# Token choice: eight rounds of the eight largest on one row per batch, norms on ScalarE, heads' weights on SP's queue

## What is computed

```python
hs = layernorm(x)                                   # (4, 512, 512)
scores = einsum('btd,d->bt', hs, w_router)
_, idx = top_k(scores, 64)                          # 64 tokens of each batch
idx = sort(idx)
sel = hs[b, idx]                                    # 256 rows in all
processed = transformer_layer(sel, rope at idx)     # 16 query heads, 8 key heads, MLP
gated = sigmoid(scores[b, idx]) * processed + (1 - sigmoid(...)) * sel
x = x + hs.at[b, idx].set(gated)
```

## Time and profile before

| what | us |
|---|---|
| median of 3 executions | 2518.43 |
| lowest, highest | 2517.94, 2521.67 |
| profiled execution: time | 2518.06 |
| profiled execution: span, first to last instruction | 2516.1 |
| busy in the span: TensorE, VectorE, ScalarE, GpSimd | 1986.4, 1068.8, 530.5, 1147.9 |
| mean granted TensorE clock | 0.893 of full speed |

### The profile page before, as it was taken

How to read it: one execution, slowest core, us unless ns; L and a number is a source line. 1 busy time by engine, 2 the same in 40 slices (tenths; PEclk the granted TensorE clock), 3 DMA queues, 4 the chain that set the end, 5 groups by cost and what they waited for, 6 DMA issues and landing times.

```text
span 2516.1 us, 33335 instructions
## 1 busy us (share of the span) xinstructions
PE 1986.4 (79%) x10460; PEld 1427.2 (57%) x10461; DVE 1068.8 (42%) x2094; ACT 530.5 (21%) x1132; POOL 1147.9 (46%) x578
## 2 busy tenths in 40 slices
PE   6925887968845789986762599999999999999910
PEld 3413443433312333333751599999999999999910
DVE  2573442057664667753840243333333333333300
ACT  3300221101102455441110121121122112112200
POOL 0000000003552655553357204776855878781886
PEclk8966997989975899999885799999999999999965
DMA  3052003221124444542135112555544545552999
GB/s 106 0 152 80 15 27 116 93 76 51 67 83 129 152 147 159 165 151 60 46 141 207 60 44 73 179 156 161 181 157 149 176 153 188 172 183 76 204 159 192
DMA packets 200086, 307.42 MB, mean 122 GB/s; under 512 B 16673, under 2 KB 95153, under 8 KB 199761
## 3 DMA queue, kind: packets, MB, share of 16 engines
q1 hardware_dynamic: 129744, 180.77, 22.6%
q0 software_dynamic: 21504, 50.74, 8.9%
q10 hardware_dynamic: 48768, 74.98, 8.9%
HBM read 188.33 MB, written 118.10 MB: 122 GB/s over the span
## 4 chain that ended last, share of the span: by engine, by line
PE 40%; issue 5%; POOL 5%; DMA 1%; DVE 1%; ACT 0%; SPq 0%; POOLq 0%; DVEq 0%; ACTq 0%
PE psum L2122 15%; PE psum L2142 8%; PE psum L2127 8%; POOL X L1748 5%; PE psum L2147 4%; PE psum L2109 3%; PE psum L2116 2%; DMA X<-d_y,f_slots 1%; DVE r_score L1915 1%; PE psum L2080 0%; PE psum L2072 0%; DMA r_w_gate<-in_L_ffn_gate_w 0%; DVE r_score L1916 0%; DVE e_gu_low L1886 0%; ACT r_hot L1767 0%
## 5 line engine op out<-in xcount | busy, mean ns | idle before, releaser
L2122 PE MATMUL psum<-e_gu_high,e_rowT_high 128*128 (+1 forms) x1272 | 430.1, 340 | 10.3 <-issue 10.2
L2122 PE MATMUL psum<-e_gu_low,e_rowT_high 128*128 (+1 forms) x1272 | 412.1, 326 | 4.0 <-issue 4.0
L1775 ACT ACTIVATE e_silu<-psum 128x352 f32<-128x352 f32 x159 | 74.0, 466 | 961.0 <-PE psum L2127 850.4
L2127 PE MATMUL psum<-e_gu_high,e_rowT_low 128*128 (+1 forms) x1272 | 258.7, 325 | 22.2 <-DVE e_rowT_low L1843 12.8
L2122 PEld LDWEIGHTS psum<-e_gu_high,e_rowT_high 128*128 128x128 f32 x1272 | 241.4, 190 | 31.5 <-issue 26.8
L2122 PEld LDWEIGHTS psum<-e_gu_low,e_rowT_high 128*128 128x128 f32 x1272 | 242.5, 191 | 8.6 <-issue 4.3
L1685 POOL TENSOR_TENSOR e_gu_high<-e_gu_in,e_ones 128x1408 fp32r<-128x1408 f32 x33 | 83.7, 2536 | 323.4 <-PE psum L2127 315.9
L2127 PEld LDWEIGHTS psum<-e_gu_high,e_rowT_low 128*128 128x128 f32 x1272 | 215.3, 190 | 23.2 <-DVE e_rowT_low L1843 13.1
L2142 PE MATMUL psum<-e_d_high,e_midT_high 128*128 (+3 forms) x477 | 190.4, 399 | 46.5 <-issue 45.6
L1852 DVE TENSOR_TENSOR e_midT_low<-psum,e_midT_high 128x256 fp32r<-128x256 f32 x159 | 67.5, 425 | 350.8 <-ACT e_midT_high L1784 323.0
L2142 PE MATMUL psum<-e_d_low,e_midT_high 128*128 (+3 forms) x477 | 189.4, 397 | 0.0
(11 more groups left out here) (338 smaller groups left out, 3693.6 us busy)
## 6 DMA issues: line engine op xcount, KB each, us to landing
d_sorted<-y_zeros SPq DMA_DIRECT2D x32, 1040.0 KB, 8.6
d_y<-e_y ACTq DMA_DIRECT2D x127, 256.0 KB
e_row<-d_sorted ACTq DMA_DIRECT2D x125, 260.0 KB
e_gu_in<-in_L_ffn_w_gate SPq DMA_DIRECT2D x32, 704.0 KB, 4.4
e_gu_in<-in_L_ffn_w_up SPq DMA_DIRECT2D x32, 704.0 KB, 5.1
e_d_in<-in_L_ffn_w_down SPq DMA_DIRECT2D x32, 512.0 KB, 4.4
d_y<-y_zeros SPq DMA_DIRECT2D x8, 1024.0 KB, 5.5
e_d_in<-in_L_ffn_w_down SPq DMA_DIRECT2D x32, 192.0 KB, 4.9
```

The lines of the kernel that those rows point to most:

```text
L2122: nc.tensor.matmul(bank[:, 0:M].unsqueeze(1), rowT_high[par][:, k, :], w[:, bass.ds(buffer, 1), k, at:at + M], start=(k == 0 and n == 0), ...
L2127: last = nc.tensor.matmul(bank[:, 0:M].unsqueeze(1), rowT_low[par][:, k, :], gu_high[:, bass.ds(buffer, 1), k, at:at + M], start=False, st ...
```

## The change

- VectorE makes one more small step, `shift` = -mean times root. ScalarE then makes the sixteen normed tiles, as X times root plus shift, and signals each; VectorE makes the score of each tile as it comes. The products' unused output goes to the eight banks and to eight parts of SBUF tables that are written later.
- The scores are turned by four transposes into one row of 512 per batch, on 4 partitions. VectorE copies the rows twice, then eight times takes the eight largest of each row (`max`) and overwrites them (`match_replace`). What differs from the copy is chosen; a scan counts the chosen, one product adds the base of the batch and clears the others. Four transposes turn the slots back, a copy of 16 columns follows, and the one-hot table is made as before.
- The trip of the scores through DRAM, the tables `before` and `tri` of this stage, the counting of larger and equal scores and the two small products are gone.
- The additions X + hs move behind the one-hot table.
- The heads' weights are issued by SP, behind the constants, without a wait.

In the diff the declarations of tiles and semaphores are left out, and some of the removed lines, which stand in the code above.

```diff
             @block.sync
             def _(sp):
                 sp.dma_start(w_router[:], c.dram["L0_ffn_w_router"].partition_broadcast(P)).then_inc(router_loaded, 16)
-                for dst, src in ((before[:], c.dram["i_before"]),
-                                 (tri[:], c.dram["i_tri"]), (iota[:], c.dram["i_iota"]), (slot_base[:], c.dram["i_slot_base"]),
+                for dst, src in ((slot_base[:], c.dram["i_slot_base"]), (iota[:], c.dram["i_count"]),
                                  (rope[:], c.dram["i_rope"].rearrange("(j p) d -> p j d", p=P)),
                                  (ln_w[:, 0], c.dram["L0_ffn_ln1_w"].rearrange("(k p) -> p k", p=P)),
                                  (ln_w[:, 1], c.dram["L0_ffn_ln2_w"].rearrange("(k p) -> p k", p=P))):
                     sp.dma_start(dst, src, allow_slow_non_contiguous=True).then_inc(loaded, 16)
-                sp.wait_ge(score_T_ready, 1)
-                sp.dma_start(c.dram["d_scores"], score_T[:]).then_inc(score_stored, 16)
-                sp.wait_ge(score_stored, 16)
-
-                sp.dma_start(scores_of_batch[:], c.dram["d_scores"].rearrange("(b j) p -> (b j p)", b=B).partition_broadcast(P)
-                             .rearrange("q (b s) -> q b s", b=B)).then_inc(scores_spread, 16)
+                for k in range(CC):
+                    rows = slice(k * P, (k + 1) * P)
+                    for src, at, cols in ((c.dram["L0_ffn_wq"], 0, QH * DH), (c.dram["L0_ffn_wk"], QH * DH, DH),
+                                          (c.dram["L0_ffn_wv"], (QH + 1) * DH, DH)):
+                        sp.dma_start(w_heads[:, k, :, at:at + cols],
+                                     src[rows, :].rearrange("p (h n) -> p h n", n=cols)).then_inc(heads_loaded, 16)
...
-                nc.gpsimd.memset(ones[:], 1.0)
+                nc.gpsimd.memset(ones[:], 1.0).then_inc(ones_set, 1)
...
                 norm_rows_into(nc, dve, chain, c, mv, rstd, var_ready, rstd_ready, 1e-5)
+                nc.vector.scalar_tensor_tensor(shift[:], mv[:, :, 0], -1.0, rstd[:], ALU.mult, ALU.mult).then_inc(shift_ready, 1)
                 dve.wait_ge(router_loaded, 16)
-                with dve.Fori(0, B) as b:
-                    tiles = [bass.ds(b * JT + j, 1) for j in range(JT)]
-                    for t in tiles:
-                        last = nc.vector.tensor_scalar(hs[:, t, :], c.X[:, t, :], mv[:, t, 0:1], rstd[:, t],
-                                                       ALU.subtract, ALU.mult)
...
-                dve.wait_ge(score_turned, 1)
-                nc.vector.tensor_copy(score_T[:], c.bank[0][0:NT, 0:P]).then_inc(score_T_ready, 1)
...
-                dve.wait_ge(scores_spread, 16)
...
-                    of_batch = scores_of_batch[:, bass.ds(b, 1), :]
-                    for j in range(JT):
-                        t = bass.ds(b * JT + j, 1)
-                        nc.vector.tensor_scalar(c.bank[j][:].unsqueeze(1), of_batch, score[:, t], None, ALU.is_gt,
-                                                ALU.add, accum_out=above[:, t])
-                        last = nc.vector.scalar_tensor_tensor(c.bank[4 + j][:].unsqueeze(1), of_batch, score[:, t],
-                                                              before[:, j:j + 1, :], ALU.is_equal, ALU.mult,
-                                                              accum_out=equal[:, t])
-                    last.then_inc(chain_dve, 1)
...
-                chain.link(nc.vector.tensor_tensor(slot[:], c.bank[1][:, 0:NT], slot_base[:], ALU.add))
-                chain.link(nc.vector.tensor_tensor(slot[:], slot[:], chosen[:], ALU.mult))
-                chain.link(nc.vector.tensor_scalar(slot[:], slot[:], -1.0, None, ALU.add))
+                unread = [bank[:] for bank in c.bank]
+                unread += [held[:, 4 * q:4 * q + 4, :].rearrange("p t s -> p (t s)") for held in (slot_hot, slot_hot_T) for q in range(4)]
+                for t in range(NT):
+                    dve.wait_ge(row_ready, t + 1)
+                    last = nc.vector.scalar_tensor_tensor(unread[t], hs[:, t, :], 1.0, w_router[:], ALU.mult, ALU.mult,
+                                                          accum_out=score[:, t:t + 1])
+                last.then_inc(score_ready, 1)
+
+                dve.wait_ge(scores_turned, 1)
+                nc.vector.tensor_copy(of_batch[:], c.bank[0][0:B, :])
+                chain.link(nc.vector.tensor_copy(left[:], c.bank[0][0:B, :]))
+                for n in range(CAP // 8):
+                    chain.link(nc.vector.max(best[:, n, :], left[:]))
+                    chain.link(nc.vector.match_replace(left[:], best[:, n, :], left[:], -3e38))
+                chain.link(nc.vector.tensor_tensor(picks[:], left[:], of_batch[:], ALU.not_equal))
+                dve.wait_ge(ones_set, 1)
+                chain.link(nc.vector.tensor_tensor_scan(slot_rows[:], ones[:], picks[:], 0.0, ALU.mult, ALU.add))
+                dve.wait_ge(loaded, 5 * 16)
+                nc.vector.scalar_tensor_tensor(slot_rows[:], slot_rows[:], slot_base[:], picks[:], ALU.add, ALU.mult).then_inc(slots_found, 1)
+
+                dve.wait_ge(slots_turned, 1)
+                chain.link(nc.vector.tensor_copy(slot[:].rearrange("p (b j) -> p b j", j=JT),
+                                                 c.bank[1][:, 0:NT].rearrange("p (j b) -> p b j", b=B)))
                 nc.vector.tensor_tensor(slot_hot[:], iota[:].unsqueeze(1).broadcast_to((P, NT, P)),
                                         slot[:].unsqueeze(2).broadcast_to((P, NT, P)), ALU.is_equal).then_inc(hot_ready, 1)
+                for t in range(NT):
+                    nc.vector.tensor_tensor(c.X[:, t, :], c.X[:, t, :], hs[:, t, :], ALU.add)
                 dve.wait_ge(gathered, 1)
...
             @block.scalar
             def _(act):
-                for k in range(CC):
-                    if k == CC // 2:
-
-                        act.wait_ge(scores_spread, 16)
-                    rows = slice(k * P, (k + 1) * P)
-                    for src, at, cols in ((c.dram["L0_ffn_wq"], 0, QH * DH), (c.dram["L0_ffn_wk"], QH * DH, DH),
-                                          (c.dram["L0_ffn_wv"], (QH + 1) * DH, DH)):
-                        act.dma_start(w_heads[:, k, :, at:at + cols],
-                                     src[rows, :].rearrange("p (h n) -> p h n", n=cols)).then_inc(heads_loaded, 16)
+                act.wait_ge(rstd_ready, 1)
+                act.wait_ge(shift_ready, 1)
+                for t in range(NT):
+                    nc.scalar.activation(hs[:, t, :], c.X[:, t, :], ACT.Identity, bias=shift[:, t:t + 1],
+                                         scale=rstd[:, t:t + 1]).then_inc(row_ready, 1)
                 act.wait_ge(gate_ready, 1)
...
             @block.tensor
             def _(pe):
-                pe.wait_ge(score_ready, B)
-                nc.tensor.transpose(c.bank[0][0:NT, 0:P], score[:], c.ident[:]).then_inc(score_turned, 1)
-
-                pe.wait_ge(chosen_ready, 1)
-                nc.tensor.matmul(c.bank[1][:, 0:NT], tri[:], chosen[:], start=True, stop=False)
-                nc.tensor.matmul(c.bank[1][:, 0:NT], ones[:], chosen_before[:], start=False, stop=True).then_inc(slot_counted, 1)
+                pe.wait_ge(score_ready, 1)
+                for j in range(JT):
+                    last = nc.tensor.transpose(c.bank[0][0:B, j * P:(j + 1) * P], score[:].rearrange("p (b j) -> p b j", j=JT)[:, :, j],
+                                               c.ident[:])
+                last.then_inc(scores_turned, 1)
+
+                pe.wait_ge(slots_found, 1)
+                for j in range(JT):
+                    last = nc.tensor.transpose(c.bank[1][:, j * B:(j + 1) * B], slot_rows[:, j * P:(j + 1) * P], c.ident[0:B, 0:B])
+                last.then_inc(slots_turned, 1)
                 pe.wait_ge(hot_ready, 1)
...
-        "i_before": np.stack([s[None, :] < (j * P + p)[:, None] for j in range(JT)], 1).astype(f),
-        "i_slot_base": np.broadcast_to(((np.arange(NT) // JT % 2) * (S // 8) + 1).astype(f), (P, NT)).copy(),
+        "i_count": np.broadcast_to((p + 1).astype(f), (P, P)).copy(),
+        "i_slot_base": (np.arange(B) % 2 * (S // 8)).astype(f)[:, None].copy(),
```

More of the change, by code:

```diff
@@ L458, in _ @@
-                chain.after_loop(B)
-                chain.link(nc.vector.tensor_tensor(above[:], above[:], equal[:], ALU.add))
-                chain.link(nc.vector.tensor_scalar(chosen[:], above[:], float(CAP), None, ALU.is_lt))
-                of = lambda tile, j: tile[:].rearrange("p (b j) -> p b j", j=JT)[:, :, j]
-                chain.link(nc.vector.memset(chosen_before[:], 0.0))
-                for j in range(1, JT):
-                    last = nc.vector.tensor_tensor(of(chosen_before, j), of(chosen_before, j - 1), of(chosen, j - 1), ALU.add)
-                    if j < JT - 1:
-                        chain.link(last)
@@ L2276 @@
```

(1 more changed line is left out.)

46 lines of the change are left out of this document (12 added, 34 removed).

## The result

The changed kernel has a median of 2497.78 us (2496.16 to 2499.49, four runs); the kernel before had 2520.05 us in the four runs beside them (2517.94 to 2525.67). The ratio is 0.9908, with a 95% interval of 0.989 to 0.9927, so 22.3 us less, and between 18 and 28. The profiled execution has a span of 2495.0 and a time of 2497.12 us. Forecast were 24.9 less and 2493.5 us, from 2489 to 2502.5.

What follows compares the result with a forecast made beforehand. One VectorE chain was taken to bound the second block's token choice; its linked steps summed to a table at 183.3 instead of 208.23 us, 24.9 less, with later stages shifting rigidly: 2493.5 us, range 2489 to 2502.5.

Steps and rivals of the forecast that it cites:

- Norms and scores: From the root, ScalarE makes sixteen rows while VectorE scores them at 0.65 us each, ending at 164.5 us.
- my upper bound: ScalarE's norm rows without overlap and with a dearer second pointer operand: 0.80 us each, adding 2.4 us.
- VectorE stays the slower: In the scoring, VectorE's 0.65 us per row sets the pace, against ScalarE's 0.60.
- Eight rounds: Choice on VectorE: eight linked rounds of MAX8 and replacement, 1.51 us each, 12.1 us together.
- Rival A: In the choice, MAX8 and replacement run at half rate like the scan: 8.5 us more, 2502.0 us, chance 0.08.
- rival B: In the choice, replacement passes over the row once per value: 29.9 us more, 2523.4 us, chance 0.02.
- The turns back: Four TensorE turns of 4 x 128 before the table: 1.04 us, bounds 0.5 less or more.
- The additions: cost 0: Sixteen additions X + hs, 9.7 us of VectorE behind the table, are covered by TensorE's gather and cost nothing.
- The weights: cost 0: Heads' weights on SP's queue land by about 185 us, 35 us before their first reader, and cost nothing.
- Rival D: Gain partly given back by ScalarE's pace (2.4), its waits (0.8), slower turns (0.5), clock (1.5 to 3): 2498 to 2501, chance 0.09.
- The 1.5 us that I allowed each way for the clock: Later stages: the granted TensorE clock may rise at another moment; one ramp is up to 3 us, 1.5 allowed each side.
- signs that I had named for "wrong": MAX8 or replacement far from 0.68 us, ScalarE rows over 0.65 apart, TensorE awaiting weights, a later stage over 3 us longer.

Runs made afterwards that it cites:

- the experiment without the cover: Changed kernel with the sixteen additions X + hs back in front of the choice, where VectorE waits for the turned scores: 2504.32 us, 9.4 above the changed kernel.
- the five later ones: Five more runs of the changed kernel, unaltered: 2494.91 us, ratio 0.9889 to the kernel before.
- that of the weights behind: Changed kernel with the heads' weights issued by ScalarE behind its sixteen norms instead of by SP: 2495.51 us, ratio 0.9894 to the kernel before.
- the norms on VectorE: Changed kernel with the sixteen normed tiles made by VectorE again: 2500.96 us, 6.1 above the changed kernel.
- the early scores: Changed kernel without score copies and one-column gather instructions, scoring products made on X one stage earlier: 2480.93 us, ratio 0.9835 to the kernel before.
- 48 more steps: Changed kernel with 48 unused MAX8 behind the eight rounds, on another chip: 2417.55 us, ratio 1.0038 to the kernel before there.
- sixteen more steps: Changed kernel with sixteen unused MAX8 behind the eight rounds, on another chip: 2396.88 us, ratio 0.9955 to the kernel before there.

## Why the prediction was right, and where its terms were off

The step that carried it, that the stage is one VectorE chain and its length is the sum of linked steps, held: 24.9 us less to the table forecast, 24.87 measured. That the sum came out so close is luck in part, since terms were off both ways.

- Norms and scores, root to last read: 11.5 us forecast (152.98 to 164.5), 12.4 measured (151.84 to 164.26). The term that was mis-sized is ScalarE's row: 0.70 us long and 0.60 apart forecast, 0.80 and (11.39 - 0.80) / 15 = 0.71 measured. The length of my upper bound, 0.80, was the true one; the rows overlap by 0.09 us where I had 0.10, so it is the length that made ScalarE the pacer. The sign of "VectorE stays the slower" was wrong, by 0.05 us per row.
- The turn of the scores: 1.3 forecast, 1.01 measured. The copies: 1.3 and 1.3.
- Eight rounds: 12.1 forecast, 178.62 - 166.68 = 11.94 measured. MAX8 of 512 is 0.68 us as taken. The replacement, which no row of before showed, is 0.66 behind a load of 0.08, with 0.07 and 0.68 forecast. Rival A (half rate) and rival B (a pass for each value) are gone. The passage of the Trainium skill on the replacement ("Vector Engine (DVE) Microarchitecture Reference", on the match/index hardware: one streaming pass behind the value load) is borne out by the 662 ns mean for 512 elements.
- Comparison, scan, product: 2.7 and 2.70. The scan of 512 was 1.21 us, from its 32-element row at twice the price per element.
- The turns back: 1.04 forecast, 0.58 measured, near my lower bound. The row that I took has 16 columns and these have four; whether that is the reason was not tested.
- The additions: cost 0, their cover named as the gather. Held, and the experiment without the cover priced it at 8.4 us to the table.
- The weights: cost 0. Held; SP was at them until 171.80 + 1.88 = 173.7 us. Issue to landing took at most 10.2 us, so they had landed by 182, 36 us ahead of the first head product, and no product with them waited for anything but the turned rows (1.66 us, as before).
- Rival D had 0.09. Of its four pieces ScalarE's pace came (0.8) and the clock came (4.5 in the cross attention of that profile), not the others. The 1.5 us that I allowed each way for the clock were too narrow. I had priced one ramp; there are dozens in the part behind, and between two profiles of the same program they differ by 4.9 us. The median of 2497.78 us lies 0.2 below the price from which D starts, so the first four runs could as well be read as D; the five later ones (2494.91) could not.
- Two of the signs that I had named for "wrong" came: ScalarE's rows further apart than 0.65 us (0.71), and a later stage grown by more than 3 us (4.5). Neither carried the time out of its range, the first because it is worth 0.8 us. B's price is 8 x 7 x 0.53 = 29.7 us and not 29.9; nothing hangs on it.

What stays open is why the cross-attention part takes 155.0 us in one execution and 162.1 in another. Reached at 716 us it took 157.5, between 735 and 739 in six profiles 160.1 to 162.1, at 751 us 157.7, from 758 to 766 in three 155.0 to 157.3, at 772 us again 160.3. Neighbours are alike, so where it falls may well matter, but there is no trend with how early it starts; what picks the pattern of the two clock levels I can't say.

"Scatter" is therefore not the whole of it: the three profiles with the changed kernel's timing (with that of the weights behind) have 160.1 to 160.5 here and the two of the kernel before 155.6 and 157.3. The part ahead of it, from the first head product on, varies as well: 512.6 to 513.1 us with the norms on VectorE, the additions first and the early scores, 515.4 to 521.3 in the other nine. So the span of a single profile says little on a few microseconds. Over the two sets of runs that have both kernels, nine of the changed one and 19 of the one before, the means are 25.0 us apart and the medians 23.5, against 24.9 at the table. If something is given back over the whole span, it is of the order of 1 us, which these runs can't tell from nothing.

## What to carry to other kernels

Where a choice of k from n runs on one engine, count its linked instructions and price each from a row with the same operand count; k / 8 rounds of MAX8 and replacement on one row per batch beat counting against all others here (the whole choice up to the table 16.8 us against 25.8, and no trip through DRAM). Look at what an idle engine could do beside the chain even where it does it slower, and keep large transfers out of the front of the list of an engine that has to compute: here twelve of them held it for 27 us. Measure a stage from its own first instruction, and believe a few microseconds at the end of the span only in medians.

## What the runs showed of the hardware

- VectorE: MAX8 of 512 elements on 4 partitions 682 ns, the replacement 662 ns with a value load of 80, the scan 1212 ns, a comparison of two rows 679; a row on 4 partitions costs what one on 128 does (a comparison on 4 679, an addition on 128 681). MAX8 and the replacement take their input from PSUM at the same price (0.69 and 0.67 us).
- ScalarE: a row of 512 from SBUF with bias and scale from SBUF is 0.80 us long and they follow at 0.71.
- Twelve transfers of 8.4 MB hold the issuing queue for 23.5 us on SP and behind the norms on ScalarE (155.01 to 178.46), and for 26.8 us in front of the norms.
- The runs of one program spread over 3 to 14 us (0.1 to 0.6%), and the profiles show by how much TensorE's level differs within a part: a mean granted clock of 0.72 to 0.76 in the cross-attention part, with 162.1 to 155.0 us for the same products.
- With sixteen and with 48 more steps, on their chip, a stretch behind 1290 us in the routed block was absent in which TensorE had been nearly idle for some 100 us. The kernel before, of which there is no trace from that chip, took 2408 us there instead of 2520. The rows are from the changed kernel and from that with sixteen more steps, columns as in the earlier trace rows. The cause is open.

```profile
1290.00:1340.00 50.00, 8.22 (x21) 6.24 (x21) 1.31 (x3) 1.58 (x4) 38.47 (x44) 0.50 0.54 208
1340.00:1390.00 50.00, 6.55 (x19) 4.76 (x19) 1.21 (x2) 0.69 (x3) 29.52 (x34) 0.50 0.43 165
```

```profile
1300.00:1350.00 50.00, 49.90 (x296) 46.50 (x295) 22.29 (x40) 13.62 (x32) 38.86 (x43) 1.00 0.66 244
```
